# A cross-feature recommender kernel: products stored even dims first, half as many row-sum matmuls, and the turn of layer 2 moved beside that of the next layer 0

## The reference

```
for i, (W, bias) in enumerate(params):            # three layers of 200 maps
    x = einsum('bhd,bmd->bhmd', h, inputs).reshape(B, -1, D)
    y = relu(einsum('oi,bid->bod', W, x) + bias[None, :, None])
    h, direct = split(y, 2, axis=1)               # last layer: direct = y
    outs.append(direct)
z = concatenate(outs, axis=1).sum(-1)             # sum over the 32 dims
h = relu(concatenate([z, dense_ctx]) @ W_top1 + b_top1)
h = relu(h @ W_top2 + b_top2)
out = h @ W_top3
```

## Time and profile before

| | |
|---|---|
| median of three runs | 2907.57 us |
| the profiled execution | 2907.22 us, span 2905.5 us |
| mean granted TensorE clock of its core | 0.993 |
| PE busy | 2830.5 us (97%), 19516 instructions |
| PEld busy | 2811.0 us (97%) |
| DVE busy | 2607.7 us (90%), 1751 instructions |
| ACT busy | 1502.0 us (52%) |
| POOL busy | 688.1 us (24%) |
| HBM over the span | 50 GB/s |

### The profile page before, as it was taken

How to read it: one execution, slowest core, us unless ns; L and a number is a source line. 1 busy time by engine, 2 the same in 40 slices (tenths; PEclk the granted TensorE clock), 3 DMA queues, 4 the chain that set the end, 5 groups by cost and what they waited for, 6 DMA issues and landing times.

```text
span 2905.5 us, 54782 instructions
## 1 busy us (share of the span) xinstructions
PE 2830.5 (97%) x19516; PEld 2811.0 (97%) x19516; DVE 2607.7 (90%) x1751; ACT 1502.0 (52%) x1880; POOL 688.1 (24%) x669
## 2 busy tenths in 40 slices
PE   2899999999999999999999999999999999999998
PEld 2899999999999999999999999999999999999996
DVE  4899999999999999999999999999999999999993
ACT  2555555555555555555555555555555555555552
POOL 2122222222222222222222222222222222222000
PEclk8999999999999999999999999999999999999999
DMA  6434333334333334333334334334333334334320
GB/s 158 101 67 100 86 74 97 86 74 98 87 74 96 87 74 99 87 74 97 87 75 98 86 74 97 87 75 96 89 73 96 88 75 99 87 75 94 95 57 21
DMA packets 280089, 249.92 MB, mean 86 GB/s; under 512 B 27803, under 2 KB 278602, under 8 KB 279965
## 3 DMA queue, kind: packets, MB, share of 16 engines
q1 hardware_dynamic: 211192, 196.57, 23.8%
q0 software_dynamic: 59744, 45.90, 11.0%
q10 hardware_dynamic: 9129, 7.13, 1.0%
HBM read 140.44 MB, written 4.20 MB: 50 GB/s over the span
## 4 chain that ended last, share of the span: by engine, by line
PE 96%; DMA 1%; SPq 1%; DVE 1%; issue 1%; ACT 0%; POOL 0%; DVEq 0%; ACTq 0%; POOLq 0%
PE acc L717 62%; PE acc L719 29%; PE z_ps L734 3%; PE hid_ps L730 1%; SPq L349 1%; PE acc L777 0%; DMA x_pairs<-x_rows 0%; DVE product L660 0%; DMA raw_weights<-in_w 0%; DVE tails L665 0%; PE hid_ps L800 0%; SPq L321 0%; DMA hid_rep<-hid 0%; POOL gathered L410 0%; DMA starts_sb<-in_table_starts 0%
## 5 line engine op out<-in xcount | busy, mean ns | idle before, releaser
L717 PE MATMUL acc<-weights,heads 126*128 126x400 f32 (+1 forms) x9088 | 2707.9, 365 | 62.3 <-DVE tails L665 62.3
L719 PE MATMUL acc<-weights,tails 126*128 126x200 f32 (+1 forms) x9088 | 2324.3, 256 | 0.0
L484 ACT ACTIVATE heads<-product 126x1024 fp32r<-126x1024 f32 (+2 forms) x1152 | 1203.9, 1048 | 1149.9 <-PE acc L719 749.5
L717 PEld LDWEIGHTS acc<-weights,heads 126*128 126x128 f32 (+1 forms) x9088 | 1717.0, 189 | 63.8 <-issue 46.6
L719 PEld LDWEIGHTS acc<-weights,tails 126*128 126x128 f32 (+1 forms) x9088 | 1744.7, 192 | 0.0
L660 DVE TENSOR_TENSOR product<-hid_rep,x_rep 126x2048 f32<-126x2048 f32 x512 | 1172.5, 2290 | 214.8 <-PE acc L719 175.5
L665 DVE TENSOR_TENSOR tails<-product,heads 126x1024 fp32r<-126x1024 f32 (+2 forms) x1152 | 1338.4, 1203 | 3.4 <-ACT heads L484 3.4
L418 POOL TENSOR_TENSOR wait_taker<-wait_taker 1x1 f32<-1x1 f32 x192 | 106.8, 556 | 2069.0 <-ACT acc_copy L490 2067.3
L410 POOL DMA_INDIRECT gathered<-in_table,rows_now x150 | 316.5, 2110 | 45.7 <-issue 45.7
L495 ACT ACTIVATE y_relu<-acc_copy 128x400 f32<-128x400 f32 x192 | 102.4, 533 | 192.8 <-DMA acc_copy<-acc_copy 192.8
L419 POOL DMA_DIRECT2D acc_copy<-acc_copy x192 | 175.8, 916 | 1.1 <-issue 0.6
(11 more groups left out here) (27 smaller groups left out, 106.4 us busy)
## 6 DMA issues: line engine op xcount, KB each, us to landing
x_rep<-x_rows SPq DMA_DIRECT2D x512, 120.0 KB
hid_rep<-hid SPq DMA_DIRECT2D x512, 120.0 KB
x_pairs<-x_rows SPq DMA_DIRECT2D x192, 280.0 KB
acc_copy<-acc_copy POOLq DMA_DIRECT2D x192, 200.0 KB
hid_rep<-hid SPq DMA_DIRECT2D x512, 5.0 KB
x_pairs<-x_rows SPq DMA_DIRECT2D x64, 120.0 KB
raw_weights<-in_w ACTq DMA_DIRECT2D x12, 492.2 KB
x_rep<-x_rows SPq DMA_DIRECT2D x128, 20.0 KB
```

The source lines that it names most:

```text
L484: act.activation(heads[0:rows, ring % HEADS_RING, 0:tiles, :], product[0:rows, ring % PRODUCT_RING, 0:tiles, :], ACT.Copy).then_inc(heads_ ...
L717: nc.tensor.matmul(acc[:, at.parity, c, 0:2 * LAYER], heads[0:rows, ring % HEADS_RING, k, cols], w, start=(q == 0 and k == 0), stop=False)
L719: last = nc.tensor.matmul(acc[:, at.parity, c, LAYER:2 * LAYER], tails[0:rows, ring % PRODUCT_RING, k, cols], w[:, 0:LAYER], start=False, ...
```

## The change

1. **Order of the columns in product, heads and tails.** DVE writes each tile's 256 columns with the 128 of even dims first and the 128 of odd dims after them. The inputs are read in their old order, so that two neighbours in the input land 128 columns (512 bytes) apart. Half c of the columns then holds the dims 2k + c of all 8 samples. ACT, the tails and PE still read whole rows or contiguous halves.
2. **Sums over dims.** A new DVE instruction, `fold`, adds the two halves of `y_relu` into `y_fold` (100 maps in layers 0 and 1, 200 in layer 2). Then `sum16`, a 128 x 8 matrix, sums 16 rows at a time, and each 100 maps need one matmul instead of two: four matmuls a block for eight.
3. **Transposes.** Each of the two now writes every second column of `hid_ps` (`c:COLS:CG`), so that the turned maps are in the old order.
4. **Placement.** turn(before) moves on PE from behind l1 q1 to behind l1 q4, directly ahead of turn(l0); its copy on ACT moves too. `y_relu` and `y_fold` have two buffers. The folds stand on DVE between the two tails at l1 q4 (before), behind the tails at l1 q6 (l0) and between the two tails at l2 q6 (l1).

```
-        y_relu = sb("y_relu", [128, CG, LAYER])
+        y_relu = sb("y_relu", [128, 2, CG, LAYER])
+        y_fold = sb("y_fold", [128, 2, LAYER])
-        sum32 = sb("sum32", [128, 128 // DIM])
+        sum16 = sb("sum16", [128, BLOCK])
...
             def relu(layer, at, b):
                 act.wait_ge(y_summed, (at.slot + 1) * 16)
-                above_zero(act, y_turned, at.slot)
-                act.activation(y_relu[:, :, :], acc_copy[:, :, 0:LAYER], ACT.Relu).then_inc(y_relued, 1)
+                above_zero(act, y_turned, at.slot - 1)
+                act.activation(y_relu[:, at.parity, :, :], acc_copy[:, :, 0:LAYER], ACT.Relu).then_inc(y_relued, 1)
...
-                dve.tensor_tensor(out, first, second, ALU.mult).then_inc(products_made, 2)
+                tiles = out.shape[1] if layer == 0 else 2 * GROUP
+                if layer > 0:
+                    out = out.rearrange("p a b c -> p (a b) c")
+                out = out.rearrange("p t (h m) -> p t m h", h=CG)
+                halved = "p t (m h) -> p t m h" if layer == 0 else "p a b (m h) -> p a b m h"
+                if layer > 0:
+                    out = out.rearrange("p (a b) m h -> p a b m h", a=2)
+                dve.tensor_tensor(out, first.rearrange(halved, h=CG), second.rearrange(halved, h=CG),
+                                  ALU.mult).then_inc(products_made, 2)
...
+            def fold(layer, at, b):
+                first = HALF if layer < 2 else 0
+                dve.wait_ge(y_relued, at.slot + 1)
+                above_zero(dve, y_turned, at.slot - 1)
+                dve.tensor_tensor(y_fold[:, at.parity, first:LAYER], y_relu[:, at.parity, 0, first:LAYER],
+                                  y_relu[:, at.parity, 1, first:LAYER],
+                                  ALU.add).then_inc(y_folded, 1)
...
                     for c in range(CG):
-                        nc.tensor.transpose(hid_ps[0:HALF, layer, c * 128:(c + 1) * 128], y_relu[:, c, 0:HALF], ident[:, :])
+                        nc.tensor.transpose(hid_ps[0:HALF, layer, c:COLS:CG], y_relu[:, at.parity, c, 0:HALF],
+                                            ident[:, :])
+                pe.wait_ge(y_folded, at.slot + 1)
                 for n, first in enumerate((HALF,) if layer < 2 else (0, HALF)):
-                    for c in range(CG):
-                        at_col = n * BLOCK + c * (BLOCK // CG)
-                        last = nc.tensor.matmul(z_ps[0:HALF, at.parity, at_col:at_col + BLOCK // CG],
-                                                y_relu[:, c, first:first + HALF], sum32[:, :], start=True, stop=True)
+                    last = nc.tensor.matmul(z_ps[0:HALF, at.parity, n * BLOCK:(n + 1) * BLOCK],
+                                            y_fold[:, at.parity, first:first + HALF], sum16[:, :], start=True, stop=True)
...
-                if l0 and before:
+                if l0 and before and before[0] < 2:
                     turn(*before)
+                    before = None
                 for q in (range(2, 5) if l0 else range(4)) if first else ():
                     accumulate(*first, q)
                 if before and not l0:
                     turn(*before)
+                if l0 and before:
+                    turn(*before)
                 if l0 and first:
                     turn(*l0)
```

More of the change, by code:

```diff
@@ L279, in where, with dims @@
             return place(layer, i - layer, (odd + layer) % 2)
+        def dims(columns, c):
+            return columns[:, c * 128:(c + 1) * 128]
         def group_tiles(layer, q):
@@ L567, in step @@
                     make_heads(*first, q)
-                if before:
+                if before and (before[0] < 2 or not l0):
                     copy_turned(*before)
+                    before = None
                 split_heads(*split_now(6))
@@ L670, in _, with make_previous_tails @@
             previous = [None]
-            def make_previous_tails(g, ring):
+            def fold(layer, at, b):
[5 more added lines that the diff above has]
+                                  ALU.add).then_inc(y_folded, 1)
+            def make_previous_tails(g, ring, between=None):
                 layer, q = previous[0]
-                for n in (2, 1):
-                    make_tails(layer, q + 2 - n, g - n, (ring - n) % RING)
+                make_tails(layer, q, g - 2, (ring - 2) % RING)
+                if between:
+                    fold(*between)
+                make_tails(layer, q + 1, g - 1, (ring - 1) % RING)
                 previous[0] = None
             def step(i, odd):
+                before, l0, l1, l2 = slots_of(i, odd)
+                first, second = (l1, l2) if l1 else (l2, None)
                 for layer in range(3):
@@ L686, in step @@
                         make_products(layer, at, q, i - layer, parity)
+                        between = None
+                        if first and layer == first[0] and q == 4 and before and before[0] > 0:
+                            between = before
+                        if second and layer == second[0] and q == 6:
+                            between = first
                         if previous[0]:
-                            make_previous_tails(at.group + q, at.ring + q)
+                            make_previous_tails(at.group + q, at.ring + q, between)
+                            if l0 and first and layer == first[0] and q == 6:
+                                fold(*l0)
                         previous[0] = (layer, q)
@@ L692, in step @@
                             make_previous_tails(at.group + 2, at.ring + 2)
+                        if before and before[0] == 0 and layer == 0:
+                            fold(*before)
                         if odd is None:
@@ L698, in _ @@
             make_previous_tails(total_groups, total_groups)
+            fold(2, place(2, blocks - 1), blocks - 1)
         @block.tensor
@@ L715, in accumulate @@
                     for c in range(CG):
-                        cols = slice(c * 128, (c + 1) * 128)
-                        nc.tensor.matmul(acc[:, at.parity, c, 0:2 * LAYER], heads[0:rows, ring % HEADS_RING, k, cols], w,
+                        nc.tensor.matmul(acc[:, at.parity, c, 0:2 * LAYER], dims(heads[0:rows, ring % HEADS_RING, k, :], c), w,
                                          start=(q == 0 and k == 0), stop=False)
-                        last = nc.tensor.matmul(acc[:, at.parity, c, LAYER:2 * LAYER], tails[0:rows, ring % PRODUCT_RING, k, cols],
+                        last = nc.tensor.matmul(acc[:, at.parity, c, LAYER:2 * LAYER], dims(tails[0:rows, ring % PRODUCT_RING, k, :], c),
                                                 w[:, 0:LAYER], start=False, stop=(q == last_q and k == tiles - 1))
```

12 lines of the change are left out of this document (8 added, 4 removed).

## The result

The changed kernel takes 3702.8 us (median of 4 runs, 3686.0 to 3722.6) against 2906.5 of the kernel before. The ratio is 1.27, its 95% interval 1.267 to 1.282. The forecast was 2866 us with a range that ended at 3200: it has the sign wrong, and the time lies 500 us above the range. The profiled execution took 3718.4 us, its span 3716.7; the mean granted TensorE clock of its core was 0.966, against 0.993 before.

The account below looks back on a forecast made before the run. PE's queue was taken to bound the kernel, with DVE hidden. 2905.5 - 46.1 (sum matmuls) + 4 (waits) + 0.5 (first steps) = 2863.9 us of span, so 2866 us; range 2855 to 3200.

Parts of the forecast that it names:

- The step that failed: DVE's products, writing to and fro between places 512 bytes apart: taken to cost the same, 2290 ns for 2048 columns.
- the upper end: DVE's products: each write takes two slots, 2.09 ns a column, +18.96 us a step.
- the 1.60 us of room: DVE's expected idle time in a step after the change: 3.19 - 0.72 - 0.87 us.
- the rival: Hopping product writes make DVE the bound from 2470 ns a product; slower, up to 3940 us; chance 0.30.
- The sums of PE: Sum matmuls on PE: 512 fewer instructions at 0.09 us, 0.72 us a block, 46.1 us in all.
- The transposes: PE's 256 transposes, writing every second column of their bank: taken to cost nothing extra.
- The rival of the slow transposes: PE's transposes take twice as long, 28 us more, giving 2894 us; chance 0.08.
- The folds: New DVE instructions: 0.25 us for 100 columns, 0.36 for 200, together 0.87 us a step.
- DVE's idle time in a step: DVE would idle 1.60 us a step instead of 3.19, so its work stays hidden.
- The new waits of PE: PE's sums wait for folds, which wait for relus: 0.06 us a step, 4 us in all.
- No gain, since DVE waits for the relu: DVE's relu waits use up its 1.60 us, so DVE sets the step: 2900 to 2910 us; chance 0.04.
- 0.58: Chance given to the forecast of 2866 us itself, with its own range of 2856 to 2880.

Follow-up runs that it names:

- e8: The changed kernel with products written in order and both inputs read with a step of two columns, two instructions a product: 2875.6 us, ratio 0.989.
- e6: The changed kernel with products written in runs of one column, alternating between halves 4 KB apart: 3721.4 us, ratio 1.278.
- e9: The kernel before with products written at a constant step of two columns, inputs read in one run, two instructions a product: 2907.9 us in one run.
- e5: The changed kernel with products written in runs of two columns, alternating between halves 4 KB apart: 2866.9 us, ratio 0.986.
- e7: e2 plus a DVE wait for each product's own semaphore before the tails: 3698.0 us.
- e11: e10 plus a DVE wait for its own product ahead of the tails: 2781.2 us, ratio 0.957.
- e2: The kernel before with only the change's product writes, even dims first; no folds, turns in their old places: 3755.8 us, ratio 1.295.
- e1: The changed kernel with its products written in one run again, as before the change: 2866.3 us, ratio 0.986.
- e10: The kernel before without the matmuls of tails on PE; DVE still makes the tails: 3168.6 us, ratio 1.090.
- e4: The changed kernel with products written in runs of 16 columns, alternating between halves 4 KB apart: 2866.8 us, ratio 0.986.

## Why the prediction was wrong

**The step that failed** is the product's: between "they cost the same" and "each write takes two slots", +18.96 us a step, it took the lower end. The price is 0.79 ns a column by the records; by the starts of a product and its tails, 3.74 us now (1409.80 to 1413.54) and 2.21 before (1021.80 to 1024.01), it is 1.53 us a product, 0.75 ns a column, 13.6 us a step. That is 72% of the upper end and some eight times the 1.60 us of room. Of the three reasons given, none decided the question: that reads stay contiguous (e8: reads may step at no cost), that the columns are as many, and that each place is filled in order (e6: it is, and it pays). They describe the pattern, not its rate. The fact nearest to it, that no two neighbours are written in a row, stood under the rival; by e9 even that does not cost by itself, only together with the going to and fro.

The Trainium skill, "Vector Engine (DVE) Microarchitecture Reference", Measured stream behaviour on trn2, had 1.71 ns a column for a destination that hops every element. The runs side with it on the whole (1.83) and against my reason for leaving it: its exception is one of a reading stream, and does not carry over to a writing one. The same section asks for at least two adjacent words; e5 agrees (2290 ns with runs of two), but e9 writes without neighbours at the full rate (1223 ns for 1024), so its rule is too wide for a constant step of two.

**The rival's price.** Its form, DVE sets the step, was right, and its point of decision, 2470 ns, was passed by far. With 13.6 us a step its sum would be 40.35 + 0.87 + 13.6 = 54.82 us, 2907 + 62 x 11.28 = 3606. The 97 us from there to 3703 no case of mine had: DVE, without pauses, delays POOL's adds and gathers, and then waits for their relus, 145 us. That this waiting is due to DVE's fullness is shown by e7 and e11 in their own kernels; how much of the 97 us in the changed kernel it makes is not measured, for the change with a gap was not run. That the changed kernel is faster than e2, though it has 56 us more on DVE, fits: its fold makes DVE wait for the relu soon, which opens the pause early, where e2 has nothing of the kind. That too is argued.

**The terms that held,** all read in e1 and e5, where the product is 2290 ns:
- The sums of PE: 512 at 0.09 us were to take 0.72 us off a step; the step went from 43.54 to 42.80.
- The transposes: the price of nothing was right but for some hundredths of a us. A pair that writes every second column takes 0.22 us in the chain of e1, as in the earlier trace rows, and 0.26 where it stands behind the sums of layer 2; twice as long would be 0.44. The rival of the slow transposes is gone. The Trainium skill, "PSUM — Partial Sum Buffer", Specifications, expects a non-contiguous pattern to slow matmuls; a step of 8 bytes doesn't in e1.
- The folds: 258 and 361 ns for 250 and 360.
- DVE's idle time in a step: 42.82 - 40.91 = 1.91 us in e1 and 2.34 in e5, where 1.60 was expected.
- The new waits of PE: 1.2 us for folds over the span, where I took 4; but the transposes wait 15.5 us for relus where they waited 10.5. The late relu holds PE one instruction earlier than I had it, and costs 6.2 us in all for 4.
- "No gain, since DVE waits for the relu": 46 us of such waits in e1, and they cost PE next to nothing: its waits for tails are 63.3 us over the span, for 62.3 before.

So the sum was right for a kernel with its products in order, and the chance was the second mistake. 0.58 rested on a term whose two ends lay 19 us a step apart, with 1.60 us of room and no row for it; the only figure at hand, 11.9 us a step, was seven times the room.

## What to carry to other kernels

An operation whose pattern the trace doesn't show, and that runs on an engine with 4% of room, decides the sign by itself: take its price in a small run of its own first, or hold the chance at what is known of it; here the one figure at hand spoke for the rival. If two streams must be parted, part them in runs of two columns instead of one; e5 is 1.4% faster than the kernel before, the same with single columns 28% slower. And when an engine is about to become the bound, look at who needs its pauses: a wait of 0.2 us behind each product was worth 387 us in e10.

## What the runs showed of the hardware

- A DVE multiplication in fp32 whose writes alternate between two places at each column takes 1.83 ns a column (3907 ns for 2048), at 512 bytes and at 4 KB; with runs of 2 or of 16 columns it takes 1.04 (2290 ns, e5 and e4). A constant step of 8 bytes is free for both reads (1221 ns for 1024) and for the write (1223 ns).
- POOL's instructions and its gathers can be held up over many DVE instructions. A gather, 1.08 us at other places, took 35.02 in e2, while DVE started 16 instructions, and a one-element addition 10.27 us in e10; both ended within 1 us after the end of DVE's work. In e10 all 64 long additions did so, in the changed kernel 17 of 57, and the others ended while DVE worked. With a DVE that waits for its own result behind each product, the longest gather was 1.36 us. The Trainium skill, "SBUF — State Buffer", Who interferes with whom, has a DVE instruction with two SBUF inputs contend with a GpSimd instruction that reads SBUF, over a port pair that one of them holds exclusively. The long additions of e10 agree, and add that the hold can last over several such DVE instructions in a row.
- DVE waiting for its own last instruction costs 0.27 us behind a hopping product (e7), which I had put at 0.1, and 0.21 behind one in order (2.41 us from a product's start to its tails' in e11, 2.20 in e10).
- A transpose into PSUM at a step of 8 bytes takes as long as a contiguous one or nearly so: 0.11 to 0.13 us in the chain of e1, for 0.11.
